# One kernel for a conv, attention and expert network on one Trainium2 core: a shorter guard, state blocks by column halves, another token layout, and one stage moved ahead

## The reference, cut to what matters

```python
h = tok(x)                                  # 9 dilated convolutions, then 64 columns
h = h + attn(layernorm(h))                  # 8 heads, full softmax attention
h = h + ffn(layernorm(h))                   # 8 experts, top 1, capacity 938
h = h + L1_attn(layernorm(h))               # phase memory, below
h = h + L1_ffn(layernorm(h))                # 6 experts, top 2, all computed

# the end of ffn: rows of the expert output are gathered back
y_tok = ybuf[idx, pos_g] * (prb * kept)[:, None]
y = nan_to_num(y_tok, nan=0.0, posinf=10000.0, neginf=-10000.0)

# L1_attn, the parts that matter here (P = 32 phases, H = 4 heads)
ao = (gelu([x, pp] @ hop_w1 + hop_b1) @ hop_w2 + hop_b2).reshape(B, L, H, P + 1)
center, width = tanh(ao[..., :P]) * PI, sigmoid(ao[..., -1:]) * 2 + 0.1
key_ph = tanh(x @ cpe_w + cpe_b) * PI
values = x @ ve_w + ve_b
gate = sigmoid(gelu(x @ sg_w1 + sg_b1) @ sg_w2 + sg_b2)
st_ph = tanh(gelu([x, cumsum(x @ kce_w + kce_b) / pos] @ ksk_w1 + ksk_b1) @ ksk_w2 + ksk_b2) * PI
# retrieval: running sums over positions of cos/sin(phase) x content and cos/sin(st_ph) x gated values,
# read with cos/sin of the query phases; the second is divided by sqrt(clip(cumsum(gate), 1)) * sqrt(P)
```

## Time and profile before

| what | value |
|---|---|
| median of 3 runs | 1361.2 us (1361.13, 1361.2, 1372.02) |
| the profiled execution | 1372.07 us |
| its span, first to last instruction | 1370.2 us, 26256 instructions |
| PE, DVE, ACT, POOL busy | 1175.9, 794.8, 641.0, 523.7 us |
| mean granted clock of TensorE | 0.891 of full |

### The profile page before, as it was taken

How to read it: one execution, slowest core, us unless ns; L and a number is a source line. 1 busy time by engine, 2 the same in 40 slices (tenths; PEclk the granted TensorE clock), 3 DMA queues, 4 the chain that set the end, 5 groups by cost and what they waited for, 6 DMA issues and landing times.

```text
span 1370.2 us, 26256 instructions
## 1 busy us (share of the span) xinstructions
PE 1175.9 (86%) x9791; PEld 751.9 (55%) x9791; DVE 794.8 (58%) x1772; ACT 641.0 (47%) x1372; POOL 523.7 (38%) x1110
## 2 busy tenths in 40 slices
PE   4769999999999999999999997290548878688998
PEld 3535566665666666666666664240335666576553
DVE  3435655665556666566565661143569898984542
ACT  0225555555555554555545543050154654743654
POOL 3021444654454544555546444307861020421200
PEclk9959999999999999999999998595557687768999
DMA  4100000000000000000000001111110000000001
GB/s 83 20 1 1 2 2 2 2 8 2 3 3 2 3 2 3 2 2 2 2 2 3 2 2 32 62 47 34 17 12 1 1 1 1 12 1 1 12 13 23
DMA packets 31322, 14.53 MB, mean 11 GB/s; under 512 B 27602, under 2 KB 28594, under 8 KB 31197
## 3 DMA queue, kind: packets, MB, share of 16 engines
q1 hardware_dynamic: 26589, 10.95, 3.4%
q0 software_dynamic: 4608, 1.91, 1.5%
HBM read 6.46 MB, written 7.27 MB: 10 GB/s over the span
## 4 chain that ended last, share of the span: by engine, by line
PE 75%; DVE 15%; issue 4%; POOL 2%; DMA 2%; ACT 1%; SPq 0%; DVEq 0%; POOLq 0%; ACTq 0%
PE psum L731 21%; PE psum L712 10%; PE psum L640 9%; PE psum L703 7%; PE psum L687 4%; PE psum L625 2%; PE psum L980 2%; PE psum L550 2%; DVE arena L1951 2%; PE psum L960 1%; PE psum L645 1%; PE psum L795 1%; PE psum L782 1%; PE psum L995 1%; PE psum L664 1%
## 5 line engine op out<-in xcount | busy, mean ns | idle before, releaser
L1399 ACT ACTIVATE arena<-psum 125x500 f32<-125x500 f32 x576 | 306.8, 585 | 338.8 <-PE psum L712 338.8
L1750 DVE TENSOR_REDUCE arena<-psum 125x1 f32<-125x500 f32 x384 | 242.6, 673 | 202.8 <-PE psum L640 202.7
L640 PE MATMUL psum<-arena 32*125 32x500 f32 (+1 forms) x1536 | 324.5, 521 | 0.6 <-ACT arena L1390 0.6
L731 PE MATMUL psum<-arena,XN 125*64 125x250 f32 x2304 | 307.9, 388 | 0.2 <-ACT arena L1399 0.2
L712 PE MATMUL psum<-arena 32*125 32x250 f32 x2304 | 291.7, 370 | 0.0
L712 PEld LDWEIGHTS psum<-arena 32*125 32x125 f32 x2304 | 214.6, 183 | 11.8 <-issue 1.0
L731 PEld LDWEIGHTS psum<-arena,XN 125*64 125x64 f32 x2304 | 140.3, 136 | 121.2 <-issue 78.6
L1753 DVE TENSOR_REDUCE arena<-psum 125x2 f32<-125x500 f32 x192 | 121.4, 674 | 71.9 <-PE psum L640 71.9
L640 PEld LDWEIGHTS psum<-arena 32*125 32x125 f32 x1536 | 128.0, 184 | 4.0 <-issue 2.2
L1175 POOL TENSOR_TENSOR lnst<-lnst,mhalf 125x12 f32<-125x12 f32 x14 | 32.0, 2284 | 244.9 <-DVE lnst L1729 244.8
L703 PE MATMUL psum<-arena,onesb 3*125 3x500 bf16 x576 | 122.4, 422 | 1.4 <-DMA arena<-arena 1.4
(11 more groups left out here) (340 smaller groups left out, 1895.2 us busy)
## 6 DMA issues: line engine op xcount, KB each, us to landing
arena<-arena SPq DMA_DIRECT2D x192, 1.5 KB
expert_in<-XN SPq DMA_DIRECT2D x8, 256.0 KB, 4.8
arena<-expert_in SPq DMA_DIRECT2D x4, 512.0 KB, 5.2
expert_out<-arena SPq DMA_DIRECT2D x4, 512.0 KB, 2.8
out<-H SPq DMA_DIRECT2D x16, 93.8 KB
expert_in<-XN,slot_in POOLq DMA_INDIRECT x48, 2.5
XN<-expert_out,slot_out POOLq DMA_INDIRECT x48, 3.9
arena<-in_L_ffn_w SPq DMA_DIRECT2D x2, 256.0 KB
```

Of the source, the lines that this page charges most:

```text
L640: last = pe.matmul(ps[0:R, at_:at_ + hi - lo], QH[row:row + 32, b, g, j * R:(j + 1) * R], KH[row:row + 32, b, g, lo:hi], start=True, stop= ...
L731: last = pe.matmul(ctx_bank[64 * h2:64 * h2 + 64, 0:THIRD], XN[:, p, c, a, :], PR[:, x % 4, h2, i * THIRD:(i + 1) * THIRD], start=(c == 0) ...
L1399: act.activation(PR[:, x % 4, h2, :], st_bank[(2 * x + h2) % 3][0:R, 0:2 * THIRD], ACT.Exp)\
L1750: dve.reduce_max(MX[:, q % 2, 0, 2 * h2 + tile:2 * h2 + tile + 1], ps[0:R, 0:2 * THIRD], AX)\
```

## The change

Four things. (1) The guard: two scalar passes put 10000 where a value is above 0 and where it is below 0, a third pass takes their difference, a fourth makes one mask of all values whose product with 0 is not 0 (infinite or not a number), and one predicated copy puts the difference there: five passes for six, with scratch in `PT`, of which only the chained ones wait for each other. (2) The state block: four products per block, each with 64 of the 128 weight columns and the 64 moving columns that belong to them, the second half to the upper output partitions, so that the result is 128 x 128 and DVE takes it with one instruction of 128 partitions; the semaphore is counted in ones, not twos. (3) Token columns: `hop2` and its bias are laid out as 2 x 128 phase columns and 2 x 4 width columns; the gate product goes behind them into the same bank; DVE empties 256 dense columns and then widths and gates together (10 columns) into a small buffer `WG` of one quarter, which ACT's sigmoids read. The first such write of a later quarter waits for the sigmoids of the one before. The weight loads on SP become four more, with pieces of 4 to 128 bytes. (4) In the list, `("hidden", 0)` comes ahead of `("gathered", 1)`; of the two only `hidden` has parts on PE and ACT, whose order therefore stays.

```diff
--- before.py
+++ after.py
@@ -44,8 +44,8 @@
 RS = 1.0 / np.sqrt(float(PP))
 
 
-GB, CVB, KSB, GTB, AOB, OB, RB2, WD, OBX = (
-    0, 8, 264, 392, 394, 658, 722, 728, 733)
+GB, CVB, KSB, TCB, WGB, OB, RB2, WD, OBX = (
+    0, 8, 264, 392, 648, 658, 722, 728, 733)
 NBIAS = 861
 
 
@@ -212,6 +212,7 @@
         WX, at = view(at, [2 * NJ * PH, WN], parts=R)
         GA, at = view(at, [6, NG], parts=R)
         hdl, at = view(at, [WN], parts=R)
+        WG, at = view(at, [NJ, 10], parts=R)
         pos1, at = view(at, [L])
         assert at <= ASIZE - 3 * 768, at
 
@@ -333,7 +334,7 @@
         todo = [("step", k) for k in range(len(steps1) + 3)]
 
         events = [("places", 0), ("gathered", 0), ("centre", 1, 0), ("variance", 1, 0), ("transpose", 1, 0), ("mean", 0),
-                  ("gathered", 1), ("hidden", 0), ("centre", 1, 1), ("variance", 1, 1), ("tokens", 0, 0), ("tokens", 0, 1),
+                  ("hidden", 0), ("gathered", 1), ("centre", 1, 1), ("variance", 1, 1), ("tokens", 0, 0), ("tokens", 0, 1),
                   ("transpose", 1, 1), ("widths", 0), ("sines", 0), ("mean", 1), ("weights", 0),
                   ("cosines", 0), ("chunk", 0)]
         for x in range(NT + 16):
@@ -498,7 +499,10 @@
             r = slice(64 * a, 64 * a + 64)
             wd += [(W["gw"][r, 8 * a:8 * a + 8], t["L0_ffn_gate_w"]),
                    (W["hop1"][r, 64 * a:64 * a + 64], t["L1_attn_hop_w1"][0:64]),
-                   (W["hop2"][r, 132 * a:132 * a + 132], t["L1_attn_hop_w2"]),
+                   (W["hop2"][r, 128 * a:128 * a + 128].rearrange("r (h c) -> r h c", c=PP),
+                    t["L1_attn_hop_w2"].rearrange("d (h c) -> d h c", c=PP + 1)[:, :, 0:PP]),
+                   (W["hop2"][r, 256 + 4 * a:256 + 4 * a + 4].unsqueeze(2),
+                    t["L1_attn_hop_w2"].rearrange("d (h c) -> d h c", c=PP + 1)[:, :, PP:]),
                    (W["wta"][r, 128 * a:128 * a + 64], t["L1_attn_mc_w"]),
                    (W["wta"][r, 128 * a + 64:128 * a + 128], t["L1_attn_ve_w"]),
                    (W["wta"][r, 256 + 32 * a:288 + 32 * a], t["L1_attn_cpe_w"]),
@@ -522,8 +526,12 @@
                      (W["hopb"][r, :], t["L1_attn_hop_b1"].unsqueeze(1))]
             for at_, name, n in ((CVB + 128 * a, "mc_b", 64), (CVB + 128 * a + 64, "ve_b", 64),
                                  (KSB + 32 * a, "cpe_b", 32), (KSB + 64 + 32 * a, "ksk_b2", 32),
-                                 (GTB + a, "sg_b2", 1), (AOB + 132 * a, "hop_b2", 132)):
+                                 (WGB + 8 + a, "sg_b2", 1)):
                 wd.append((bias[:, at_:at_ + n], t["L1_attn_" + name].partition_broadcast(128)))
+            b2 = t["L1_attn_hop_b2"].rearrange("(h c) -> h c", c=PP + 1)
+            wd.append((bias[:, TCB + 128 * a:TCB + 128 * a + 128].rearrange("r (h c) -> r h c", c=PP),
+                       b2[:, 0:PP].partition_broadcast(128)))
+            wd.append((bias[:, WGB + 4 * a:WGB + 4 * a + 4].unsqueeze(2), b2[:, PP:].partition_broadcast(128)))
         for at_, name, n in ((GB, "L0_ffn_gate_b", 8), (OB, "L1_attn_out_b", 64), (RB2, "L1_ffn_router_b2", 6)):
             wd.append((bias[:, at_:at_ + n], t[name].partition_broadcast(128)))
         wd.append((W["b1"][:, :], t["L0_ffn_b1"].rearrange("e (h f) -> f (e h)", h=2)))
@@ -843,11 +851,11 @@
                     own = slice((i - p // 2 * 2 * NJ) * R, (i - p // 2 * 2 * NJ + 1) * R)
                     ps, done = take(pe, ("tok", i))
                     pe.matmul(ps[0:R, 0:320], XT[:, cols], W["wta"], start=True, stop=True)
-                    pe.matmul(ps[0:R, 320:384], KG[:, own], W["ksk2"], start=True, stop=True)
-                    pe.matmul(ps[0:R, 384:386], SG[0:64, own], W["sg2"][0:64, :], start=True, stop=True)\
+                    pe.matmul(ps[0:R, 320:384], KG[:, own], W["ksk2"], start=True, stop=True).then_inc(done, 1)
+                    ps, done = take(pe, ("ao", i))
+                    pe.matmul(ps[0:R, 0:264], HG[:, own], W["hop2"], start=True, stop=True)
+                    pe.matmul(ps[0:R, 264:266], SG[0:64, own], W["sg2"][0:64, :], start=True, stop=True)\
                         .then_inc(done, 1)
-                    ps, done = take(pe, ("ao", i))
-                    pe.matmul(ps[0:R, 0:264], HG[:, own], W["hop2"], start=True, stop=True).then_inc(done, 1)
 
             def gate_sums(p):
                 pe.wait_ge(S["gate"], p + 1)
@@ -881,8 +889,9 @@
                 if j < NJ - 1:
                     ps, done = take(pe, ("state", x))
                     for a in range(2):
-                        last = pe.matmul(ps[:, a * 128:(a + 1) * 128], FF[:, g + a, :],
-                                         CV[:, g // 2, a].rearrange("r c d -> r (c d)"), start=True, stop=True)
+                        for c in range(2):
+                            last = pe.matmul(ps[64 * c:64 * c + 64, a * D:(a + 1) * D], FF[:, g + a, 64 * c:64 * c + 64],
+                                             CV[:, g // 2, a, c, :], start=True, stop=True, tile_position=(0, 64 * c))
                     last.then_inc(done, 1)
 
             def retrieved(x):
@@ -891,7 +900,7 @@
                 emptied(pe, ("sm", x, 0))
                 emptied(pe, ("sm", x, 1))
                 if j:
-                    pe.wait_ge(S["state"], 2 * (p * (NJ - 1) + j))
+                    pe.wait_ge(S["state"], p * (NJ - 1) + j)
                 ps, done = take(pe, ("ret", x))
                 for a in range(2):
                     o = ps[0:R, a * D:(a + 1) * D]
@@ -1476,10 +1485,10 @@
                     emptied(act, ("ao", i))
                 for x in phases_of(p, TC, TK):
                     act.activation(x, x, ACT.Tanh).then_inc(S["tanh"], 1)
-                ws = WS[:, 48 * p:48 * p + 48]
-                act.activation(ws, ws, ACT.Sigmoid).then_inc(S["width"], 1)
+                act.activation(WS[:, 48 * p:48 * p + 48].rearrange("r (n c) -> r n c", c=8), WG[:, :, 0:8], ACT.Sigmoid)\
+                   .then_inc(S["width"], 1)
                 g = slice(2 * NJ * p, 2 * NJ * (p + 1))
-                act.activation(GA[:, 0, g], GA[:, 1, g], ACT.Sigmoid).then_inc(S["gate"], 1)
+                act.activation(GA[:, 0, g].rearrange("r (n c) -> r n c", c=2), WG[:, :, 8:10], ACT.Sigmoid).then_inc(S["gate"], 1)
 
             def window(p):
                 act.wait_ge(S["warg"], p + 1)
@@ -1846,12 +1855,12 @@
                 w = pk.rearrange("r (a n j) -> r a n j", a=2, n=NP)[:, :, p, :].rearrange("r a j -> r j a")
                 link(dve.tensor_tensor(XN[:, p], XN[:, p], w.unsqueeze(3).to_broadcast([R, NJ, 2, D]), ALU.mult))
 
-                link(dve.tensor_scalar(msk, yf, 3.4028235e38, None, ALU.is_gt))
-                link(dve.copy_predicated(yf, mski, big[0:R, 0:1].to_broadcast([R, 768])))
-                link(dve.tensor_scalar(msk, yf, -3.4028235e38, None, ALU.is_lt))
-                link(dve.copy_predicated(yf, mski, big[0:R, 1:2].to_broadcast([R, 768])))
-                link(dve.tensor_tensor(msk, yf, yf, ALU.not_equal))
-                link(dve.copy_predicated(yf, mski, zero1[0:R, 0:1].to_broadcast([R, 768])))
+                above, below = (PT.rearrange("r n g h p -> r (n g h p)")[:, 768 * n:768 * n + 768] for n in range(2))
+                dve.tensor_scalar(above, yf, 0.0, 1.0e4, ALU.is_gt, ALU.mult)
+                link(dve.tensor_scalar(below, yf, 0.0, 1.0e4, ALU.is_lt, ALU.mult))
+                dve.tensor_tensor(above, above, below, ALU.subtract)
+                link(dve.tensor_scalar(msk, yf, 0.0, 0.0, ALU.mult, ALU.not_equal))
+                link(dve.copy_predicated(yf, mski, above))
                 link(dve.tensor_tensor(pairs(H, p), pairs(H, p), y, ALU.add))
 
 
@@ -1884,15 +1893,13 @@
                     dve.tensor_tensor(CV[:, n].rearrange("r a c d -> r (a c d)"), ps[0:R, 0:256],
                                       bias[0:R, CVB:CVB + 256], ALU.add)
                     dve.tensor_tensor(TK[:, n].rearrange("r k a p -> r (k a p)"), ps[0:R, 256:384],
-                                      bias[0:R, KSB:KSB + 128], ALU.add)
-                    dve.tensor_tensor(GA[:, 1, 2 * i:2 * i + 2], ps[0:R, 384:386], bias[0:R, GTB:GTB + 2], ALU.add)\
-                       .then_inc(done, 1)
+                                      bias[0:R, KSB:KSB + 128], ALU.add).then_inc(done, 1)
                     ps, done = filled(dve, ("ao", i))
-                    v = ps[0:R, 0:264].rearrange("r (g c) -> r g c", c=PP + 1)
-                    bv = bias[0:R, AOB:AOB + 264].rearrange("r (g c) -> r g c", c=PP + 1)
-                    dve.tensor_tensor(TC[:, 2 * n:2 * n + 2].rearrange("r g h p -> r (g h) p"), v[:, :, 0:PP],
-                                      bv[:, :, 0:PP], ALU.add)
-                    dve.tensor_tensor(WS[:, 8 * i:8 * i + 8].unsqueeze(2), v[:, :, PP:], bv[:, :, PP:], ALU.add)\
+                    dve.tensor_tensor(TC[:, 2 * n:2 * n + 2].rearrange("r g h p -> r (g h p)"), ps[0:R, 0:256],
```

(20 more changed lines are left out.)

## The result

| | before | changed |
|---|---|---|
| median | 1363.09 us (6 runs, 1359.72 to 1372.02) | 1352.51 us (6 runs, 1351.63 to 1355.22) |
| ratio to before | | 0.9923, 95% interval 0.9898 to 0.9948 |
| profiled execution, span | 1372.07, 1370.2 us | 1352.31, 1350.3 us |

A forecast was written before the change was run, and what follows sets the result against it. No engine is full until 1032 us, DVE leads to 1220, then PE. Terms -5.4 - 3.2 - 4.2 - 1.0 + 2.1 = -11.7 us take the median 1361.2 to 1349.5 us; 8-in-10 range 1340 to 1358 us.

The forecast's parts named there:

- Order, -5.4 forecast: From 925 to 1032 us: earlier hop additions and POOL's queue let the gate scale start 5.4 us earlier.
- the near end of the bounds: For the gate scale behind POOL's gathers: 5.4 us taken, from 0 if gathers are slowed to 5.5 if not.
- The second rival: Gathers stretch beside moved DVE work, gate scale not earlier: sum -6.3 us, 1355 us; chance 0.20.
- The sign of being wrong that I had named: On POOL: a last gather ending after 1016 us; the gate scale was expected near 1014 us.
- The 1.0 us won at L1175: POOL idled 1.02 us before L1175, waiting for DVE; the shorter guard moves its whole queue 1.0 us ahead.
- Guard, -3.2 forecast: Five DVE passes for six save 1.6 us a quarter; quarters 2 and 3 count, 3.2 us.
- State on DVE, -4.2: One DVE instruction for two saves 0.32 us per block; 13 of 20 blocks count, 4.2 us.
- State on PE, +2.1: Eight instructions for four cost PE 0.3 us more in 7 blocks, 2.1 us; bounds -2.8 and +5.
- The third rival: State products on PE run alone with the array standing still: 1.1 us per block, +8 us, 1369 us; chance 0.06.
- Token columns, -1.0: One 2-column DVE eviction less per tile, 0.07 us in 18 tiles, counted as 1.0 us; bounds 0 and 1.7.
- The last stage is only shifted.: From 1220 us on PE is busy 134 of 151 us, so a microsecond taken from DVE gains nothing there.
- The sign I had named: From 1032 to 1220 us: a mean clock, 0.74 before, moved by over 0.05 would be time in no term.

The follow-up runs named there:

- the second measurement: The changed kernel run again with no edit, against the kernel before: 1353.39 us against 1361.46, ratio 0.9935.

## Why the prediction was right, and where not

The size came out (10.6 us for 11.7; 8.1 in the second measurement), and its case too: within 1% and not above. The time itself, 1349.5 us, was 3.0 us too low (1352.51), 1.9 us of them because the median of before was 1361.2 us in three runs and 1363.09 in six. Of the terms not all came out, so part of the agreement is luck.

- **Order, -5.4 forecast.** The mechanism is right and shown from both sides: the token side gains ten, the gathers' queue lets half through, and with the queue out of the way 8.7 us more appear. The size fell short: 3.5 us alone, 0 to 2 beside the guard. The step that failed is the choice of the near end of the bounds, "since the stretch before also had DVE work in it". The second rival's mechanism is real: gathers beside DVE's long passes take up to 2.3 us. I let it decide fully or not at all, and priced it with 1.61 us a gather. The twelve gathers of quarter 3 took 1.4 us more than 12 x 1.27 before, and 1.9 and 3.6 us more in the two profiles of the changed kernel; the gate scale came 4.5 and 2.0 us earlier, for 5.4. The sign of being wrong that I had named, a last gather ending after 1016 us, is met in the second profile (88.0 + 1.56 after the first gather, so 1017.1 on the scale of the forecast) and not in the first (1014.6). The 1.0 us won at L1175 was 0.6 (32.3 against 32.9 us after the first gather).
- **Guard, -3.2 forecast.** Undersized. A quarter saves 1.8 us, not 1.6, and alone the guard gives 6.6 us by medians, since without the new order quarter 1's also stands on the path. The forecast booked that share, of the 4.5 us that POOL waited for DVE, under the order.
- **State on DVE, -4.2.** 0.32 us a block is exact; by the table DVE's instruction gives 2.5 us in the DVE stage, so about 8 blocks counted, not 13.
- **State on PE, +2.1.** The sign was wrong. The trace had shown the pair L995 at work side by side; I took the middle between that and one after the other, and the near row was right: 0.23 us less per block at the low clock and 0.07 at the high one. So for both engines together -2.1 us had been forecast and -2.2 (-3.0 by the ratio) was measured alone, from a gain and a loss that were both put too high; that the sum fits is luck. The third rival has nothing behind it. The rule that a change of tiling mode drains the array (Trainium skill, "TensorEngine Tiling (Array Packing)", "Key Properties") shows here at most as the 0.17 us by which the next product is later. The rule in the same place that different tiles can work in parallel is what the trace agrees with: four products in 0.62 us, where one with 64 moving columns takes 0.31 to 0.42 us from start to start.
- **Token columns, -1.0.** 1.6 by medians, zero inside the interval; no more can be said.
- **"The last stage is only shifted."** This failed. Of 3.2 us that the state blocks gain up to the last chunk 2.8 are gone at the end, with PE at its low clock for longer. The sign I had named, a middle stage whose mean clock moves by more than 0.05, doesn't settle it: 0.69 for 0.74 in the first profiles, 0.70 for 0.71 in the second ones.

The wrong terms ran against each other: the PE term was at least 2.1 us too dear, the guard was too cheap, DVE's state term, order and last stage too hopeful. The page "SBUF — State Buffer" of the Trainium skill, section "Who interferes with whom", has a rule that bears on the order: a DVE pass with two SBUF inputs contends with a GpSimd instruction that reads SBUF, and in a two-port mode DVE and GpSimd exclude each other. The trace agrees in part: gathers of 1.27 us with DVE quiet, up to 2.29 beside pairs of two-tensor passes of 2.35 us, but one of 1.27 beside such a pair too. The same section says that two-tensor passes had not stalled DMAs issued by GpSimd; here they stand beside the longest gathers, and the measurement decides.

## What to carry to other kernels

When work is moved ahead, look at which hand-written queue releases its consumer, and move that entry too: here the one line without its counterpart in POOL's queue gave 3.5 us alone and 0 to 2 beside the guard, and the counterpart 8.7. When two changes shorten the same wait, book it once. Beside gathers issued by POOL, count long DVE passes on two tensors as a possible cost to the gathers. And take two profiles before trusting a stage whose clock stands between its two levels: 5 us lay in it here.

## What the runs showed of the hardware

- A gather's issue on POOL takes 1.27 us with DVE quiet and up to 2.29 us beside DVE passes with two tensors in SBUF. One program shows 85.7 and 88.0 us from the start of the first to that of the last gather in two executions.
- DVE pays as well: in the changed kernel's first quarter one scalar pass of 768 elements, begun while the gather from 944.54 to 945.81 us was under way, took 1.04 us, where its neighbour took 0.56:

```profile
944.65 0.56 DVE L1859 TENSOR_SCALAR arena<-XN 125x768 f32<-125x768 f32 x1
945.13 1.04 DVE L1860 TENSOR_SCALAR arena<-XN 125x768 f32<-125x768 f32 x1
```


- Four products with 64 output columns each, two in each of the two column halves, at 64 moving columns: 8 instructions in 0.62 us at the low clock, where 4 instructions with 128 output and 128 moving columns take 1.02 us; 0.38 for 0.55 us at the high clock.
